# Repartitioning the routed experts of a transformer layer, and a separate path for the last batch

## The chip, the cores and the metric

One core of a Trainium2 chip runs the whole layer. The metric is the device time of one execution in microseconds (us), the median of several. PE is the tensor engine, PEld its weight loads, DVE the vector engine (VectorE), ACT the scalar engine (ScalarE), POOL GpSimd, SP the sync engine that issues most DMAs. Each engine runs its own list of instructions in order and waits on semaphores.

## The reference

`x` has 8 batches of 512 tokens of 128 values, in fp32. The layer is:

```python
x = x + attention(layernorm(x))
x = x + ffn(layernorm(x))

def attention(x):   # 16 heads
    y = einsum('bnd,hde->bhne', x, Wkqv) + bkqv       # k, q: 128 wide, v: 8 wide
    k, q, v = y[..., :128], y[..., 128:256], y[..., 256:]
    A = softmax(where(tril, q @ k.T / sqrt(128), -inf))
    return (A @ v, heads side by side) @ Wp + bp

def ffn(x):         # 8 experts of inner width 256, top 2 of a sigmoid router, and a shared expert
    shared = (silu(x @ shared_gate.T) * (x @ shared_up.T)) @ shared_down.T
    scores, idx = top_k(sigmoid(x @ router_w.T + routing_bias), 2); scores /= sum(scores)
    return shared + sum over the two experts e of score_e * (silu(x @ gate_w[e]) * (x @ up_w[e])) @ down_w[e]
```

## The kernel before

The program after a short preparation is one list of 215 slots `t` (`for t in range(SLOTS)` on each engine). Slots 0 to 127 project the 128 pairs of batch and head (`project`, three matmuls of 512 columns, since each operand is split into a high and a low fp16 half) and find row maxima (`score_for_max` on PE, `reduce_maxima` on DVE). Ten slots later (`LAG`) the pair's scores are made and exponentiated in three tiles (`score`, ACT line 1256), Pool masks the diagonals (lines 904 and 906), and every fourth slot (t = 15, 19, ...) `weigh_values` multiplies four heads with the values in fp32 (line 1032); ACT stores the products to `o_dram`. Attention so ends at slot 139. `FFN_AT` is 138.

For each batch a train of small steps follows, at slots that `STEPS` gives relative to 29 + 16 b: SP gathers sums and products from `o_dram` (`gather_products`, lines 796 and 797), DVE inverts the sums (`rinv`), SP stores the inverses and reads them back broadcast (`spread_inverses`, lines 801 and 806), Pool multiplies (`mult`, line 913), PE projects (`proj`), DVE adds and takes the variances by bn_stats and three Newton steps (`stats`, `aggr`, `newton0` to `newton2`), Pool normalizes (`norm`, line 920), ACT and DVE split the rows in two fp16 halves (`split`), SP stores them to `x_dram` and reads them back transposed (`turn_rows`, lines 810 and 819), and PE makes the logits of the router (`logits`, lines 1059 to 1061), of which ACT takes the exponential at once. Batch 7 has a table of its own, `LAST_STEPS`; its norm is on DVE.

Tokens are routed in three parts. `SPLITS` counts tiles of 128 tokens, four to a batch: (0, 8), (8, 20), (20, 32), that is 2, 3 and 3 batches. For each part DVE picks the two best experts of each token (`sort_at`, seven pieces, 13 operations, at two slots), PE counts and ranks them (`count`, `rank`), DVE turns ranks into rows (`place`), and Pool scatters the rows by indirect DMA into `xs_dram`, sorted by expert (`sends_at`, planned by `plan_sends`, line 929). SP reads them transposed, in quads of four tiles, into a ring of `X_RING` = 4 quads (line 865); for the first quad of a part it waits until all rows of the part are sent, and each quad waits for `gate_up` of the quad four before.

The feed-forward has 69 units, one in a slot from 138 to 206: 15, 19 and 19 of parts 0, 1 and 2 (each unit is 256 rows of one expert: 12 matmuls of 256 columns, lines 1099 to 1101) and 16 of the shared expert (each is half the inner width of a batch: 6 matmuls of 512 columns). The order was part 0, part 1, three shared batches, part 2, five shared batches (`ORDER`, `SHARED_ORDER`). ACT takes SiLU (line 1287) and the high half (1292), DVE the product (1546) and the low half (1549); `LATE` = 4 slots after its unit PE does the down-projection (lines 1135 to 1137). PE may be three units ahead (`DEEP`). ACT stores the experts' output to `ys_dram`. Pool gathers each token's two rows back by indirect DMA from slot `FETCH_AT` of the part on, three gathers in two slots (`plan_fetches`, lines 938 and 942), each pair waiting for `gate_up`. DVE adds the shared product of a batch (line 1541), and the weighted rows (`combine`, line 1517): tiles of all but the last part at planned slots, those of the last part after the slots. SP stores the output by batches in order (line 869).

One bank of PSUM (`bank_t`, bank 7) serves all small products in turn (`T_USES`, `turn`).

## Time and profile before

| | us |
|---|---|
| median of 3 runs | 767.33 (763.23 to 767.85) |
| the profiled execution | 765.89 |
| its span, first to last instruction | 764.1 |
| PE busy | 659.3 (86%) |
| VectorE busy | 538.8 (71%) |
| ScalarE busy | 459.9 (60%) |
| Pool busy | 304.5 (40%) |

The span is what the engines' rows cover; the profiled execution's own time is 1.8 us longer. Busy shares are means over stages that have different limits, so the rows below are read by stage.

### The profile page before, as it was taken

The numbers are of one execution on the slowest core, as the hardware profiler recorded it, in microseconds if no ns is written. First come the engines' busy times: TensorE is split into PE (matmuls) and PEld (weight loads), VectorE is DVE, ScalarE is ACT, GpSimd is POOL, SyncE is SP. The second block draws the span as 40 slices with busy tenths as digits, with TensorE's granted clock in tenths as the row PEclk, the third lists the DMA queues.
The fourth block names the chain that finished last, engine by engine and source line by source line (L and its number), as shares of the span: only waits on it lengthen the run. The fifth ranks groups of instructions, "written<-read, shape, count | busy, mean of one in ns | idle before, by whom it ended". The sixth has DMA issues, their size and how long they took to land. (4 is left out here: it accounts for less than half of the span.)

```text
span 764.1 us, 16403 instructions
## 1 busy us (share of the span) xinstructions
PE 659.3 (86%) x5426; PEld 398.2 (52%) x5426; DVE 538.8 (71%) x1900; ACT 459.9 (60%) x817; POOL 304.5 (40%) x508
## 2 busy tenths in 40 slices
PE   7478999999989998999999998996788789888920
PEld 6354455545545554454555554553377677577610
DVE  6799777787788788878778778762057755667914
ACT  3366667757757766667867766673475546556600
POOL 3493512314223223463322322367600067666671
PEclk9799999999999999999999999999899899999955
DMA  9102335411110311230210210134155543764322
GB/s 249 46 2 64 90 108 149 144 57 57 46 56 29 74 36 36 75 114 26 80 51 29 59 32 28 40 78 103 36 120 113 113 108 111 142 120 123 101 67 83
DMA packets 104849, 61.07 MB, mean 80 GB/s; under 512 B 45960, under 2 KB 96544, under 8 KB 104768
## 3 DMA queue, kind: packets, MB, share of 16 engines
q1 hardware_dynamic: 68336, 29.34, 15.9%
q10 hardware_dynamic: 32336, 22.29, 9.5%
q0 software_dynamic: 4096, 8.40, 4.3%
q8 instruction: 47, 0.77, 0.4%
q14 instruction: 34, 0.28, 0.1%
HBM read 19.88 MB, written 31.06 MB: 67 GB/s over the span
## 5 line engine op out<-in xcount | busy, mean ns | idle before, releaser
L1256 ACT ACTIVATE p_sb<-bank,inv_scale 128x512 f32<-128x512 f32 (+1 forms) x384 | 221.9, 614 | 34.3 <-PE bank L1018 27.1
L1370 DVE CUSTOM_DVE_ANT_0 junk<-bank,causal 128x512 bf16<-128x512 f32 (+3 forms) x512 | 221.2, 483 | 23.6 <-PE bank L995 23.3
L904 POOL TENSOR_SCALAR_AFFINE_SELECT p_sb<-p_sb 128x384 f32<-128x384 f32 x128 | 66.9, 522 | 303.5 <-ACT p_sb L1256 303.3
L1017 PE MATMUL bank<-ql,ah 128*128 128x512 f16 (+3 forms) x512 | 153.7, 300 | 0.0
L1018 PE MATMUL bank<-qh,al 128*128 128x512 f16 (+3 forms) x512 | 153.2, 300 | 0.0
L995 PE MATMUL bank<-ah,qh 128*128 128x512 f16 (+3 forms) x512 | 132.1, 302 | 23.6 <-DVE low L1370 22.2
L1016 PE MATMUL bank<-qh,ah 128*128 128x512 f16 (+3 forms) x512 | 147.5, 301 | 1.2 <-ACT p_sb L1256 1.2
L1342 DVE TENSOR_TENSOR ql<-bank,qh 128x512 f16<-128x512 f32 x128 | 88.5, 691 | 68.9 <-ACT qh L1221 65.2
L1221 ACT ACTIVATE qh<-bank 128x512 f16<-128x512 f32 x128 | 76.4, 597 | 63.3 <-PE bank L960 61.7
L1546 DVE SCALAR_TENSOR_TENSOR al<-bank,gu_scale,ah 128x512 f32<-128x512 f32 x69 | 51.6, 748 | 72.9 <-ACT ah L1287 56.6
L995 PEld LDWEIGHTS bank<-ah,qh 128*128 128x128 f16 x512 | 50.0, 98 | 82.2 <-DVE low L1370 49.7
L929 POOL DMA_INDIRECT xs_dram<-rows,place x64 | 65.8, 1028 | 60.4 <-DVE place L1507 41.0
L1287 ACT ACTIVATE ah<-bank,inv_gate 128x512 f32<-128x512 f32 x69 | 47.4, 687 | 62.8 <-PE bank L1101 44.6
L1032 PE MATMUL bank<-p_sb,v_sb 128*9 128x512 f32 (+3 forms) x1024 | 78.0, 446 | 7.3 <-POOL p_sb L906 7.3
L1016 PEld LDWEIGHTS bank<-qh,ah 128*128 128x128 f16 x512 | 50.2, 98 | 42.1 <-issue 9.5
L938 POOL DMA_INDIRECT p_sb<-ys_dram,place x57 | 59.4, 1042 | 30.6 <-issue 13.1
L1246 ACT ACTIVATE oT<-bank 128x512 f32<-128x512 f32 x32 | 19.1, 598 | 78.7 <-PE bank L1032 78.7
L1135 PE MATMUL bank<-wh,qh 128*128 (+1 forms) x276 | 52.7, 225 | 15.1 <-issue 7.3
L1099 PE MATMUL bank<-mh,wh 128*128 128x256 f16 x212 | 60.6, 286 | 3.7 <-issue 3.3
L1018 PEld LDWEIGHTS bank<-qh,al 128*128 128x128 f16 x512 | 50.2, 98 | 25.1 <-issue 0.4
L1100 PE MATMUL bank<-ml,wh 128*128 128x256 f16 x212 | 60.6, 286 | 2.7 <-issue 2.7
L1101 PE MATMUL bank<-mh,wl 128*128 128x256 f16 x212 | 60.5, 285 | 1.8 <-issue 1.7
(234 smaller groups left out, 1162.0 us busy)
## 6 DMA issues: line engine op xcount, KB each, us to landing
o_dram<-oT ACTq DMA_DIRECT2D x32, 256.0 KB, 2.3
ys_dram<-ql ACTq DMA_DIRECT2D x25, 256.0 KB
xs_dram<-causal ACTq DMA_DIRECT2D x6, 832.0 KB, 4.6
wst<-in_Wkqv SPq DMA_DIRECT2D x8, 264.0 KB, 5.3
x_sb<-in_x SPq DMA_DIRECT2D x8, 256.0 KB, 6.0
o_all<-o_dram SPq DMA_DIRECT2D x8, 256.0 KB
r_all<-r_dram SPq DMA_DIRECT2D x8, 256.0 KB
x_dram<-rows SPq DMA_DIRECT2D x8, 256.0 KB, 2.3
```

The costliest lines, as they stand in the source:

```text
L904: nc.gpsimd.affine_select(out=three, in_=three, compare_op=ALU.is_ge, fill=0.0, base=0, pattern=[[0, 3], [1, P]], channel_multiplier=-1).t ...
L929: nc.gpsimd.indirect_dma_start(out=m.xs_dram[g], out_offset=bass.IndirectOffsetOnAxis(ap=place[:, k, i:i + 1], axis=0), in_=rows[:, i // T ...
L995: last = nc.tensor.matmul(m.psum[M_BANK[n % 2]][:, at:at + w], qh[:, u % RING, i * P:(i + 1) * P], m.ah[:, seg(b, N, w)], start=True, stop ...
L1016: nc.tensor.matmul(bank, m.ah[:, keys], qh[:, s, c * P:N], start=True, stop=False)
L1017: nc.tensor.matmul(bank, m.ah[:, keys], ql[:, s, c * P:N], start=False, stop=False)
L1018: last = nc.tensor.matmul(bank, m.al[:, keys], qh[:, s, c * P:N], start=False, stop=True)
L1032: last = nc.tensor.matmul(m.psum[O_BANK][32 * j:32 * j + V1, c * P:N], m.v_sb[:, v // H * TB + c, v % H, :], p_sb[v % P_RING][:, P_AT[c]:P ...
L1099: nc.tensor.matmul(out, hi, x_h, start=True, stop=False)
L1221: nc.scalar.activation(qh[:, t % RING, :], m.psum[Q_BANK][:, :], ACT.Copy).then_inc(qh_ready, 1)
L1256: nc.scalar.activation(p_sb[v % P_RING][:, S_AT[k]:S_AT[k] + S_WIDTH[k]], m.psum[S_BANK[k]][:, 0:S_WIDTH[k]], ACT.Exp, scale=m.inv_scale[: ...
L1342: nc.vector.tensor_tensor(ql[:, t % RING, :], m.psum[Q_BANK][:, :], qh[:, t % RING, :], ALU.subtract).then_inc(ql_ready, 1)
L1370: last = nc.vector.tensor_tensor_reduce(out=junk[:, (3 * u + k) % 2, at:at + w], in0=m.psum[M_BANK[(3 * u + k) % 2]][:, at:at + w], in1=m. ...
```

## The change

- `SPLITS` becomes (0, 12), (12, 24), (24, 32): parts of 3, 3 and 2 batches, so 19, 19 and 15 units. All eight shared batches come behind the last part. Part 2 is at slots 176 to 190, the shared units at 191 to 206. The scatters of part 0 move from slots 76 to 83 to 88 to 99 (24 for 16), those of part 1 from 124 to 135 to 138 to 153, those of part 2 from 159 to 174 (24) to 157 to 167 (16). The 64 gathers move from slots 175 to 219 to 168 to 210. The last part's row additions after the slots are those of 8 tiles, not 12.
- Steps of batches 0 to 6: `rinv`, `mult` and `proj` two slots earlier, `aggr` and `newton0` in the slot of `stats`, `norm` three slots earlier, `split` and `logits` four slots earlier (batch 6's logits two, at 141). The exponential of batch 6's logits is taken with batch 7's, at slot 152; `lg` gets two buffers.
- The sorts of parts 0 and 1 are spread over five slots (`SORT_LATE`) instead of two.
- Batch 7: at slot 144 Pool itself issues the two gathers from `o_dram`, the store of the inverses and their broadcast, and waits for each in its own list. Its normalized rows are turned by four fp32 transposes on PE (slot 150, `late`), and ACT and DVE split them from PSUM straight into `xh` and `xl` (slot 151, `late_copy`); `x_dram` is not used for it. `split`, which makes the rows for the scatter, comes after the logits.
- SP: batch 6's rows are stored and turned at the fifth quad as before; the gathers, the broadcast and the turn of batch 7 are gone from its list.

```diff
...
 GU_BOUND = 32.0 / W_BOUND ** 2
-SPLITS = ((0, 8), (8, 20), (20, 32))
+SPLITS = ((0, 12), (12, 24), (24, 32))
 PARTS = len(SPLITS)
...
 PLACE_LATE = -(-(PV_AT - LOW_AT) // GROUP)
-STEPS = {"rinv": 2, "mult": 4, "proj": 6, "stats": 6, "aggr": 8, "newton0": 10, "newton1": 10, "newton2": 10, "norm": 11, "split": 14, "logits": 18}
-LAST_STEPS = {"rinv": 1, "mult": 4, "proj": 6, "stats": 6, "aggr": 6, "newton0": 7, "newton1": 7, "newton2": 7, "norm": 7, "split": 8, "logits": 13}
-PART_STEPS = {"sort": 22, "weigh": 26, "count": 27, "rank": 30, "place": 30, "expert": 34, "send": 31}
-LAST_PART_STEPS = {"sort": 14, "count": 16, "weigh": 16, "rank": 17, "place": 17, "expert": 18, "send": 18}
+STEPS = {"rinv": 0, "mult": 2, "proj": 4, "stats": 6, "aggr": 6, "newton0": 6, "newton1": 7, "newton2": 7, "norm": 8, "split": 10, "logits": 14}
+LATE_LOGITS = 16
+LAST_STEPS = {"rinv": 3, "mult": 3, "proj": 7, "stats": 7, "aggr": 7, "newton0": 8, "newton1": 8, "newton2": 8, "norm": 8, "late": 9, "late_copy": 10, "logits": 11, "split": 12}
+PART_STEPS = {"sort": 18, "weigh": 22, "count": 23, "rank": 26, "place": 26, "expert": 30, "send": 27}
+LAST_PART_STEPS = {"sort": 12, "weigh": 13, "count": 14, "rank": 15, "place": 15, "expert": 16, "send": 16}
+SORT_LATE = ((0, 0, 0, 1, 2, 3, 4), (0, 0, 0, 0, 1, 1, 1))
...
+    if (name, b) == ("logits", B - 2):
+        return step_at("rinv", b) - STEPS["rinv"] + LATE_LOGITS
     return PV_AT + H - GROUP + 2 + H * b + (STEPS if b < B - 1 else LAST_STEPS)[name]
...
-    return part_step_at("sort", g) + k // 4 * (GROUP if g < PARTS - 1 else 1)
+    return part_step_at("sort", g) + SORT_LATE[g == PARTS - 1][k]
...
     return next((b for b in range(B) if step_at(name, b) == t), None)
+
+
+def late_at(name, t):
+
+    return step_at(name, B - 1) == t
...
                 + [(SHARED_T_AT + k, "shared", k) for k in range(2)]
-                + [(step_at(name, b), name, b) for name in ("proj", "logits") for b in range(B)]
+                + [(step_at(name, b), name, b) for name in ("proj", "logits") for b in range(B)] + [(step_at("late", B - 1), "late", 0)]
                 + [(part_step_at(name, g), name, g) for name in ("count", "rank") for g in range(PARTS)])
...
 X_RING, GU_RING, LATE, DEEP = 4, 6, 4, 3
-ORDER = ("part", 0), ("part", 1), ("shared", 3), ("part", 2), ("shared", 5)
+ORDER = ("part", 0), ("part", 1), ("part", 2), ("shared", 8)
 SHARED_ORDER = (6, 5, 0, 7, 1, 2, 3, 4)
...
 quad_ends = [max(u + 1 for u, unit in enumerate(units) if unit.quad is quad) for quad in quads]
-LAST_TURN = next(q for q in range(X_RING, len(quads)) if FFN_AT + quad_ends[q - X_RING] >= step_at("split", B - 1))
 T_LAST = max(t for t, _, _ in T_USES)
...
-            def turn_rows(b):
+            def store_rows(b):
                 sp.wait_ge(xl_ready, b + 1)
                 sp.dma_start(m.x_dram[b * N:(b + 1) * N, :].rearrange("(t p) d -> p t d", p=P), rows[:, b % HN_RING, :, :]).then_inc(x_stored, 16)
+
+            def turn_rows(b):
                 sp.wait_ge(x_stored, 16 * (b + 1))
...
                         load_weights(e)
-                for b in range(B):
+                for b in range(B - 2):
                     if step_at("split", b) < LOW_AT + GROUP * g <= step_at("split", b) + GROUP:
+                        store_rows(b)
                         turn_rows(b)
...
                 if q == X_RING:
+                    store_rows(B - 2)
                     turn_rows(B - 2)
-                    gather_products(B - 1)
-                if q == X_RING + 1:
-                    spread_inverses(B - 1)
-                if q == LAST_TURN:
-                    turn_rows(B - 1)
                 if q >= X_RING:
...
+                if late_at("rinv", t):
+                    for k in range(2):
+                        pool.wait_ge(o_stored[k], 16 * H // GROUP // 2 * B)
+                    pool.wait_ge(rinv_ready, B - 1)
+                    pool.wait_ge(on_ready, B - 1)
+                    heads = m.o_dram[(B - 1) * H // GROUP * P:B * H // GROUP * P, :].rearrange("(h c) n -> h c n", h=H)
+                    pool.dma_start(sums[:, :], heads[:, DH, :]).then_inc(late_sums_placed, 16)
+                    pool.dma_start(o_all[:, :], heads[:, 0:DH, :]).then_inc(late_o_placed, 16)
+                    pool.wait_ge(rinv_ready, B)
+                    pool.dma_start(m.r_dram[(B - 1) * P:B * P, :], rinv[:, :]).then_inc(late_r_stored, 16)
+                    pool.wait_ge(late_r_stored, 16)
+                    inverses = m.r_dram[(B - 1) * P:B * P, :].rearrange("(h c) n -> h (c n)", h=H)
+                    pool.dma_start(r_all[:, :], inverses.unsqueeze(1).to_broadcast([H, DH, N])).then_inc(late_r_placed, 16)
+                if late_at("mult", t):
+                    pool.wait_ge(late_r_placed, 16)
+                    pool.wait_ge(late_o_placed, 16)
                 if (b := batch_at("mult", t)) is not None:
-                    pool.wait_ge(r_placed, 16 * (b + 1))
-                    pool.wait_ge(o_placed, 16 * (b + 1))
+                    pool.wait_ge(r_placed, 16 * min(b + 1, B - 1))
+                    pool.wait_ge(o_placed, 16 * min(b + 1, B - 1))
                     if b >= 1:
...
                     last.then_inc(t_filled, 1)
+                if late_at("late", t):
+                    turn("late", 0)
+                    pe.wait_ge(hn_ready, B)
+                    for i in range(TB):
+                        last = nc.tensor.transpose(bank_t[:, i * P:(i + 1) * P], hn[:, i, :], m.ident[:, :])
+                    last.then_inc(t_filled, 1)
                 if (b := batch_at("logits", t)) is not None:
...
                         pe.wait_ge(scale_chain, SCALE_LINKS)
-                    pe.wait_ge(x_turned, 16 * 2 * (b + 1))
+                    if b < B - 1:
+                        pe.wait_ge(x_turned, 16 * 2 * (b + 1))
                     for i in range(TB):
...
                 if unit.shared:
-                    if unit.half == 0:
+                    if unit.half == 0 and unit.batch < B - 1:
                         pe.wait_ge(x_turned, 16 * 2 * (unit.batch + 1))
+                    elif unit.half == 0:
+                        pe.wait_ge(t_taken, T_TURN["late", 0] + 1)
                     for kind, bank in ((0, GB), (1, UB)):
...
                     act.dma_start(m.ys_dram[quad.part][quad.rows, :].rearrange("(j p) d -> p j d", p=P), yst[:, q % X_RING, 0:quad.n * D].rearrange("p (j d) -> p j d", d=D)).then_inc(ys_stored[q % X_RING], 16)
+                if late_at("late_copy", t):
+                    act.wait_ge(t_filled, T_TURN["late", 0] + 1)
+                    act.wait_ge(wl_ready, KINDS * (E + 1))
+                    nc.scalar.activation(xh[:, seg(B - 1, N)], bank_t[:, :], ACT.Copy, scale=LIFT).then_inc(late_xh_ready, 1)
                 if t >= FFN_AT:
                     split_rows(t)
-                if (b := batch_at("logits", t)) is not None:
-                    act.wait_ge(t_taken, T_TURN["logits", b] + 1)
-                    nc.scalar.activation(ex[:, seg(b, TB), :], lg[:, :, :], ACT.Exp, scale=-1.0).then_inc(ex_ready, 1)
+                for b in range(B):
+                    if step_at("logits", max(b, B - 1) if b == B - 2 else b) == t:
+                        act.wait_ge(t_taken, T_TURN["logits", b] + 1)
+                        nc.scalar.activation(ex[:, seg(b, TB), :], lg[:, b % 2, :, :], ACT.Exp, scale=-1.0).then_inc(ex_ready, 1)
...
                     dve.wait_ge(t_filled, T_TURN["logits", b] + 1)
-                    if b >= 1:
-                        dve.wait_ge(ex_ready, b)
-                    nc.vector.scalar_tensor_tensor(out=lg[:, :, :], in0=bank_t[:, 0:TB * E].rearrange("p (t e) -> p t e", e=E), scalar=m.inv_logit[:, :],
+                    if b >= 2:
+                        dve.wait_ge(ex_ready, b - 1)
+                    nc.vector.scalar_tensor_tensor(out=lg[:, b % 2, :, :], in0=bank_t[:, 0:TB * E].rearrange("p (t e) -> p t e", e=E), scalar=m.inv_logit[:, :],
                                                    in1=m.rb_bc[:, :].unsqueeze(1).to_broadcast([P, TB, E]), op0=ALU.mult, op1=ALU.add).then_inc(t_taken, 1)
...
                     nc.vector.tensor_copy(ranks[:, 0:n], bank_t[:, 0:n]).then_inc(t_taken, 1)
+                if late_at("late_copy", t):
+                    dve.wait_ge(late_xh_ready, 1)
+                    dve.wait_ge(t_filled, T_TURN["late", 0] + 1)
+                    dve.wait_ge(wl_ready, KINDS * (E + 1))
+                    nc.vector.scalar_tensor_tensor(out=xl[:, seg(B - 1, N)], in0=bank_t[:, :], scalar=LIFT, in1=xh[:, seg(B - 1, N)], op0=ALU.mult, op1=ALU.subtract).then_inc(t_taken, 1)
                 if (b := batch_at("split", t)) is not None:
...
                 if (b := batch_at("rinv", t)) is not None:
-                    dve.wait_ge(sums_placed, 16 * (b + 1))
+                    if b < B - 1:
+                        dve.wait_ge(sums_placed, 16 * (b + 1))
+                    else:
+                        dve.wait_ge(late_sums_placed, 16)
                     if b >= 1:
...
                     nc.vector.reciprocal(rinv[:, :], sums[:, :]).then_inc(rinv_ready, 1)
...
```

## Rows read from the trace of the kernel before

**Rows 1.** stretches: busy us of each engine (instructions), granted clock, DMA share, GB/s

```profile
core 0: us, PE busy (x) PEld busy (x) DVE busy (x) ACT busy (x) POOL busy (x), PEclk, DMA share, GB/s
509.60:544.40 34.80, 26.46 (x209) 14.65 (x209) 6.65 (x35) 19.96 (x36) 26.61 (x40) 0.95 0.33 94
560.30:612.00 51.70, 41.45 (x423) 34.24 (x421) 33.87 (x89) 29.80 (x48) 1.27 (x1) 0.87 0.55 120
650.00:704.00 54.00, 46.56 (x499) 37.77 (x500) 35.18 (x64) 29.31 (x53) 34.48 (x34) 1.00 0.61 129
704.00:726.00 22.00, 21.39 (x210) 14.12 (x208) 20.50 (x42) 15.30 (x28) 14.28 (x14) 1.00 0.40 105
726.00:753.00 27.00, 6.06 (x35) 2.99 (x32) 3.46 (x9) 0.55 (x1) 17.37 (x19) 0.53 0.21 57
```

**Rows 2.** timeline, ScalarE's copies of slots 67 to 69, 87, 88 (start, duration)

```profile
271.78 0.60 ACT L1221 ACTIVATE qh<-bank 128x512 f16<-128x512 f32 x1
...
279.26 0.60 ACT L1221 ACTIVATE qh<-bank 128x512 f16<-128x512 f32 x1 [1.64 <-PE bank L960]
...
282.21 0.60 ACT L1221 ACTIVATE qh<-bank 128x512 f16<-128x512 f32 x1 [0.38 <-PE bank L960]
...
352.95 0.60 ACT L1221 ACTIVATE qh<-bank 128x512 f16<-128x512 f32 x1 [0.57 <-PE bank L960]
...
358.15 0.60 ACT L1221 ACTIVATE qh<-bank 128x512 f16<-128x512 f32 x1 [0.25 <-PE bank L960]
```

**Rows 3.** timeline, SiLUs of slots 143, 144, 159, 178, 180, 200, 201, 206

```profile
560.30 0.69 ACT L1287 ACTIVATE ah<-bank,inv_gate 128x512 f32<-128x512 f32 x1 [0.65 <-PE bank L1101]
...
568.03 0.69 ACT L1287 ACTIVATE ah<-bank,inv_gate 128x512 f32<-128x512 f32 x1
...
612.08 0.69 ACT L1287 ACTIVATE ah<-bank,inv_gate 128x512 f32<-128x512 f32 x1 [1.66 <-PE bank L1101]
...
660.59 0.69 ACT L1287 ACTIVATE ah<-bank,inv_gate 128x512 f32<-128x512 f32 x1 [4.35 <-remote]
...
667.20 0.69 ACT L1287 ACTIVATE ah<-bank,inv_gate 128x512 f32<-128x512 f32 x1 [4.30 <-PE bank L1101]
...
712.03 0.69 ACT L1287 ACTIVATE ah<-bank,inv_gate 128x512 f32<-128x512 f32 x1 [0.27 <-PE bank L1101]
...
713.99 0.69 ACT L1287 ACTIVATE ah<-bank,inv_gate 128x512 f32<-128x512 f32 x1 [0.48 <-issue]
...
724.41 0.69 ACT L1287 ACTIVATE ah<-bank,inv_gate 128x512 f32<-128x512 f32 x1 [0.28 <-PE bank L1101]
```

**Rows 4.** the chain of waits, its end (start, duration)

```profile
734.05 18.66 another core or an unknown queue
```

**Rows 5.** timeline, Pool's gathers of the last part: first and last of 24

```profile
718.66 0.94 POOL L938 DMA_INDIRECT p_sb<-ys_dram,place  x1 [3.75 <-PE bank L1101]
...
747.91 0.94 POOL L942 DMA_INDIRECT p_sb<-ys_dram,place  x1 [0.30 <-issue]
```

**Rows 6.** timeline, VectorE at the end

```profile
755.03 6.38 DVE L1517 SCALAR_TENSOR_TENSOR x_sb<-p_sb,weight,x_sb 128x128 f32<-128x128 f32 x24
```

**Rows 7.** timeline, PE's last group: first, 22nd and 23rd of 24

```profile
733.01 0.29 PE L1135 MATMUL bank<-wh,qh 128*128 128x128 f16 x1 [3.33 <-DVE qh L1549]
...
751.93 0.29 PE L1135 MATMUL bank<-wh,qh 128*128 128x128 f16 x1 [0.44 <-issue]
752.63 0.27 PE L1136 MATMUL bank<-wh,qh 128*128 128x128 f16 x1 [0.41 <-issue]
```

**Rows 8.** timeline, Pool between attention and feed-forward

```profile
544.12 3.13 POOL L920 TENSOR_SCALAR hn<-x_sb,stats,rstd 128x128 f32<-128x128 f32 x4
...
571.34 1.27 POOL L913 TENSOR_TENSOR onT<-o_all,r_all 128x512 f32<-128x512 f32 x1 [23.36 <-DMA r_all<-r_dram]
```

**Rows 9.** timeline, PE at the logits of batch 6

```profile
563.37 0.17 PE L1059 MATMUL bank<-rwh,xh 128*128 128x8 f16 x1 [2.44 <-DMA xl<-x_dram]
```

**Rows 10.** timeline, SP's broadcast of the inverses of batch 7

```profile
567.92 0.53 SPq L806 DMA_DIRECT2D r_all<-r_dram  x1
```

More of the change, by code:

```diff
@@ L715, in body @@
     tmp = sb("tmp2", [P, TB], F32)
-    lg = sb("lg", [P, TB, E], F32)
+    lg = sb("lg", [P, 2, TB, E], F32)
     ex = sb("ex", [P, TILES, E], F32)
@@ L753, in body @@
              "half_added", "out_ready", "out_stored",
-             "xn_ready", "xn_last_ready", "x_T", "ah_ready", "al_ready", "v_done", "v_ready", "mh_ready", "ml_ready", "scale_chain")
+             "xn_ready", "xn_last_ready", "x_T", "ah_ready", "al_ready", "late_xh_ready", "late_sums_placed", "late_o_placed", "late_r_stored", "late_r_placed", "v_done", "v_ready", "mh_ready", "ml_ready", "scale_chain")
     (q_done, qh_ready, ql_ready, max_scored, max_ready, low_stored, low_placed,
@@ L761, in body @@
      half_added, out_ready, out_stored,
-     xn_ready, xn_last_ready, x_T, ah_ready, al_ready, v_done, v_ready, mh_ready, ml_ready, scale_chain) = (sem(n) for n in names)
+     xn_ready, xn_last_ready, x_T, ah_ready, al_ready, late_xh_ready, late_sums_placed, late_o_placed, late_r_stored, late_r_placed, v_done, v_ready, mh_ready, ml_ready, scale_chain) = (sem(n) for n in names)
     o_stored = [sem(f"o_stored{k}") for k in range(2)]
```

## The prediction

> **What bounds the kernel now.** I read the views in this order: the stretches (busy time by stage), the end of the chain of waits, the SiLU rows of ScalarE as a clock of the feed-forward slots, and then the Pool and SP rows at the points where that clock stops. The span is 764.1 us, and the profiled execution took 765.89 us, 1.8 more. The reader is to see three regimes in [rows 1]. In attention PE sets the pace as long as there are projections: a plain slot takes 2.95 us and a slot with a value product 5.20 [rows 2]. In the last ten slots before the feed-forward (509.6 to 544.4) PE is busy 26.5 of 34.8 us and Pool 26.6: Pool's 18 scatters of part 1, two in a slot, hold the masks back. From slot 138 on PE issues the next unit as soon as it may. Undisturbed, a slot is 1.96 us (712.03 to 713.99 in [rows 3]), so 68 slots would take 133 us; they take 180 (544.4 to 724.41). After the last SiLU at 724.41 come 39.7 us in which almost nothing is computed: PE executes 35 matmuls in 27 us [rows 1], VectorE stands for 18.66 us in the chain [rows 4], Pool issues the last gathers at one in 1.25 us [rows 5], and 24 row additions of 6.38 us follow [rows 6].
>
> **The tail.** In the old plan part 2 (12 tiles, 24 gathers) is computed last but for five shared batches; its first gather runs at 718.66 and its last at 747.91 [rows 5]. In the new plan part 2 has 8 tiles and ends at slot 190, all eight shared batches stand behind it, and the 64 gathers are laid on slots 168 to 210 in place of 175 to 219. At most six gathers are left when the last but one gate/up product is done: 6 x 1.25 = 7.5 us from some 1.5 us before the last SiLU. VectorE has 16 additions left, 16/24 of 6.38 = 4.3 us. What stands between is PE. Its last down-projection is 24 matmuls, the first at 733.01 and the last but one at 752.63 [rows 7], against 1.31 us for such a group at full pace (an estimate: two undisturbed slots of 1.96 hold twelve matmuls of 512 columns and this group's 24 of 128, which are a third of the columns). Instructions start there 0.70 us apart (751.93, 752.63) or a multiple of it, for no wait that the profile shows. I have to say what makes this crawl. Rows for Pool as the cause: in 560.3 to 612, with Pool silent (one instruction), no such gap stands; they begin with the scatters at 613 and come in bursts through 650 to 704; and they are dense while gathers run back to back. Rows against: 704 to 726 has 14 Pool instructions and no gap at all (PE 21.4 of 22.0) [rows 1]. I take Pool as the cause. The crawl then ends with the last gather's landing. By 747.91 to 752.63 that is some 4 us after the last issue, so 7.5 - 1.5 + 4 = 10 us after the last SiLU; then a rest of the group, 1.5; the two additions of shared products, 1.5; row additions 4.3; output 2.9 (end of the additions 761.4 to 764.1). Tail: 20.2 us in place of 39.7, **-19.5**. If the crawl belongs to the last instructions of PE's program and not to Pool, it stays: then only 8 row additions (2.1) and a little are saved, -3.
>
> The Trainium skill ("Runtime: NRT & Kernel Launch", Instruction fetch mechanics) says that instruction fetch is mostly hidden and that PE holds some 2,048 instructions. By it the end of the program can't starve and the crawl is not the program's; the trace doesn't decide that. It goes with the choice above and changes no number.
>
> **Slots 128 to 137.** With part 1 ending at batch 5 as before, but its ranks known at slot 135 in place of 123, its 24 scatters move from slots 124 to 135 to 138 to 153. Pool is left with masks of about 0.8 us a slot, one product and one normalization (3.13 us [rows 8]) three slots earlier. The next limit is PE: 26.5 us of work in those slots, some of it waiting inside, or ScalarE with 20.0. I take 24 us for the ten slots (bounds 20 and 30): **-10.8**. **Start of the feed-forward.** At 544.12 the normalization of batch 6 stood ahead of the last masks; from 544.4 to 560.30 [rows 3] five slots took 15.9 us for 9.8. With it at slot 133 I leave 1 us: **-5**. **Logits of batch 6.** PE waited 2.44 us for the turned rows [rows 9] and ScalarE then loaded two tables; the slot took 7.73 us (560.30 to 568.03). Split at 135, logits at 141 with SP idle before it, and the exponential drawn to slot 152 remove all of it: **-5.7** (at least -4, as PE's order keeps its 12 small matmuls).
>
> **Attention.** Four slots (67, 71, 115, 119) carry 7 to 11 small VectorE operations at once: 279.26 - 271.78 = 7.48 against 5.20 [rows 2], 2.3 each; the rank and place slots add 1 to 1.5 each. In all about 14 us for two parts. The new sorts are spread over 79 to 83, and those of part 1 fall on 127 to 131, where VectorE has little else. Slot 83 gets stats, seed, sort and weights together (+2). I keep 5 of 14 for part 0: **-8** (bounds -2 and -11). The step table for each batch moves reciprocal and products two slots earlier and stacks stats, variance and the first Newton step; a wash: what slot 40 loses, slots 33, 35 and 36 gain. The gathers of products are issued at the same point of SP's list, and land about 2 us ahead of the new reciprocal, so no new wait.
>
> **Batch 7.** Removed are SP's two gathers, the store and the broadcast, x_dram's store and two turns. Added are four Pool DMAs, four fp32 transposes on PE and two copies. Pool reaches slot 144 at about gate_up 5, one scatter behind; it waits for the reciprocal, for the store and for the broadcast before it goes on, and everything behind it, 15 scatters of part 1, waits too. No row shows a plain Pool DMA. Its issue I put at the indirect one's 1.25 us [rows 5]; the flight of the broadcast at SP's, issue 567.92 to product 571.34, 3.4 us [rows 8, 10]. Lower bound: as on SP (0.5 us of issue); upper: 2 us of issue and 5 of flight each. Sum from Pool at slot 144: 1.25 + 2.5 (sums), 0.5 reciprocal (VectorE is there at the same time, +2), 1.25 + 2, 1.25 + 3.4, 1.27 product: 15 us, against 5 slots or so of PE (144 to 148, 11 us with its own stalls). PE's projection waits **+3** (0 to +12). Transposes, copies and their bubbles cost **+1.5**; the round trip through x_dram that they replace lay under slots 149 to 153 and gives nothing back by itself, but the last place is ready two slots earlier. The stalls of the chain from projection to place (560.30 to 612.08, 16 slots, 51.8 us for 31.4, of which logits of batch 6 are counted above) stay: the Newton steps, the table loads, the sorts. The 15 scatters that Pool still owes after the product need 15 x 1.28 = 19 us and are done as PE comes to slot 157, which the chain itself makes late: 24 scatters in the feed-forward bring bursts, of which I take **+3** outside other stalls.
>
> The Trainium skill ("DMA: Bandwidth & Descriptors", Latency and other measured facts) speaks against this move: first byte about 0.6 us on SP's path and 1 us on Pool's. By that alone four transfers would lose 1.6 us on the chain; no row here shows it, and the 3 above doesn't contain it.
>
> **Part 2 and the gathers.** 16 scatters for 24, at 0.4 us each (612.08 to 667.20: 55.1 us for 21 slots, 14 over, with 24 scatters and ten gathers in them): **-3**. The SiLUs of slots 178 and 180 began after 4.35 and 4.30 us of idle on ScalarE (660.59, 667.20), because part 2's rows were sent until 650; in the new plan they are sent by slot 168 for slot 176: **-5**. From 667.20 to 724.41 26 slots took 57.2 us, 6.2 over, with 1.5 gathers in each; 12 more slots carry them now: **+4**.
>
> **Sum.** -19.5 -10.8 -5 -5.7 -8 +3 +1.5 +3 -3 -5 +4 = -45.5 us from 765.9: 720.4. The profiled execution lies 1.4 us below the median of 767.33, so the forecast for the median is **722 us**.
>
> **Rivals.** (1) The crawl stays. For it: the gaps keep a beat of 0.70 us whatever Pool's beat is, PE's program ends there, and 704 to 726 shows Pool without crawl. The tail gives -3 in place of -19.5: **738 us**. (2) The chain of batch 7 is late on Pool. The waits at slot 144 reach the upper bound, the scatters of part 1 are pushed behind slot 157, and PE stands for them: +9 and +6: **737 us**. (3) The change does not do what it says in attention: the slots 128 to 137 are bound by the ping-pong of scores and exponentials near 3 us a slot, and stats, variance and Newton in slots 35 and 36 take back what the sorts gave: +6 and +8, **736 us**. (4) Slower: Pool becomes the bound of the whole feed-forward. It has 40 scatters and 64 gathers after slot 138 in place of 88 DMAs and the four waits; they need 104 x 1.28 = 133 us of 180. It decides only if the blocked time at slot 144 passes 15 us and each Pool DMA then costs PE 0.7 us more than now: 104 x 0.7 = 73, 722 + 73 - 20 = **775 us**.
>
> **Chances.** Forecast 0.58, with its own range 708 to 733; rivals (1) 0.17, (2) 0.08, (3) 0.09, (4) 0.03; 0.05 is left for a mixture near no change. The range 705 to 744 leaves out 2 in 10: the lower end adds 4 in attention, 4 in slots 128 to 137, and a last group of PE that doesn't crawl at all (8); the upper takes in rivals 1 to 3 with some room. What a measurement of this kernel tells from no change is about 1%, 8 us. Faster by more: 0.92; within: 0.04; slower: 0.04.
>
> **What would show it.** The first SiLU near 525 us, and that of slot 143 some 11 us later; no table load for an exponential before slot 152; Pool's product for batch 7 within 3 us of PE's need; unit 206's SiLU near 700; the last gather issued 6 us after it and the end 20 us after it. Wrong would be: gaps of 0.70 us after the last gather has landed, PE waiting at slot 157 for transposed rows, or the ten slots before the feed-forward still above 3 us each.

## The result, and the profile after

The changed kernel takes 742.18 us (740.01 to 742.48, 4 runs) against 767.38 us: a ratio of 0.967, 95% interval 0.9632 to 0.9708. It is faster, inside the forecast range of 705 to 744, and 20 us above the 722 that I forecast. The profiled execution took 742.48 us, its span is 740.7. Of all executions in this document one is left out: one of the four with denser scatters (below) took 958.41 us at a mean granted clock of 0.652, against 0.963 to 0.967 in the other three.

Three stretches, cut at the first and the last SiLU, against the terms of my sum (from 764.1 of span to 740.7):

| stretch | before | after | difference | my terms |
|---|---|---|---|---|
| start to first SiLU (slot 138) | 544.4 | 533.3 | -11.1 | -18.8 |
| first to last SiLU (slot 206) | 180.0 | 186.8 | **+6.8** | -7.2 |
| last SiLU to the end | 39.7 | 20.6 | -19.1 | -19.5 |

The tail came out as long as I had worked out; the feed-forward, where I expected a gain, got longer. One profile fixes these stretches to some us only: a second one of the same kernel (744.52 us, the first run on the first kind below) has 531.5, 193.5 and 17.7. The feed-forward is longer than before in both, by 6.8 and 13.5 us. By stretches of the kernel after (busy us of each engine and its instructions; PEclk is the granted clock), to be held against [rows 1]:

```profile
core 0: us, PE busy (x) PEld busy (x) DVE busy (x) ACT busy (x) POOL busy (x), PEclk, DMA share, GB/s
502.20:533.30 31.10, 29.50 (x265) 16.38 (x261) 17.22 (x72) 22.68 (x39) 13.47 (x30) 1.00 0.34 86
533.30:561.80 28.50, 24.39 (x273) 19.54 (x266) 16.75 (x33) 14.65 (x27) 14.31 (x16) 1.00 0.51 120
564.00:576.00 12.00, 5.05 (x32) 3.00 (x33) 2.87 (x14) 1.06 (x2) 7.46 (x9) 0.66 0.19 59
606.90:686.70 79.80, 69.71 (x733) 59.17 (x734) 45.83 (x81) 44.34 (x79) 49.26 (x48) 0.94 0.62 132
720.10:740.70 20.60, 6.11 (x65) 4.72 (x62) 12.18 (x33) 1.95 (x4) 6.66 (x7) 0.61 0.42 115
```

The first line runs from slot 127 to the first SiLU, one slot more than the first line of [rows 1]; the same cut takes 40.0 us in the kernel before, with Pool busy for 29.4. Pool's work has become 13.5 us and PE is busy in 29.5 of 31.1, so the scatters no longer hold the masks back and PE is the limit. The third line is a new loss: 32 matmuls in 12 us. Pool's rows and, with them, the two SiLUs of slots 149 and 150 (start, duration; in brackets the idle time before and what ended it):

```profile
546.66 0.61 POOL L921 DMA_DIRECT2D sums<-o_dram  x1
547.28 0.56 POOL L922 DMA_DIRECT2D o_all<-o_dram  x1
551.54 0.58 POOL L924 DMA_DIRECT2D r_dram<-rinv  x1 [3.70 <-DVE rinv L1471]
554.47 0.53 POOL L927 DMA_DIRECT2D r_all<-r_dram  x1 [2.35 <-DMA r_dram<-rinv]
557.87 1.27 POOL L936 TENSOR_TENSOR onT<-o_all,r_all 128x512 f32<-128x512 f32 x1 [2.87 <-DMA r_all<-r_dram]
559.30 1.39 POOL L952 DMA_INDIRECT xs_dram<-rows,place  x1 [0.16 <-issue]
561.00 0.99 POOL L952 DMA_INDIRECT xs_dram<-rows,place  x1 [0.30 <-issue]
...
572.41 0.96 POOL L952 DMA_INDIRECT xs_dram<-rows,place  x1 [0.30 <-issue]
```

```profile
559.29 1.13 PE L1072 MATMUL bank<-wp,onT 128*128 128x128 f32 x8 [0.72 <-POOL onT L936]
```

```profile
561.76 0.69 ACT L1319 ACTIVATE ah<-bank,inv_gate 128x512 f32<-128x512 f32 x1 [2.86 <-PE bank L1131]
575.54 0.69 ACT L1319 ACTIVATE ah<-bank,inv_gate 128x512 f32<-128x512 f32 x1 [10.87 <-remote]
```

The chain of batch 7 on Pool, which I feared, costs PE 0.72 us of waiting. Then Pool works off its scatters, eleven back to back, most of them 1.27 us apart. PE waits once for VectorE in that time (1.21 us), and then does this, for no wait that the profile shows ("issue"):

```profile
568.98 0.42 PE L1129 MATMUL bank<-mh,wh 128*128 128x256 f16 x1
569.81 0.37 PE L1130 MATMUL bank<-ml,wh 128*128 128x256 f16 x1 [0.41 <-issue]
570.53 0.37 PE L1131 MATMUL bank<-mh,wl 128*128 128x256 f16 x1 [0.36 <-issue]
571.95 0.38 PE L1129 MATMUL bank<-mh,wh 128*128 128x256 f16 x1 [1.05 <-issue]
```

After the first row starts are 0.83, 0.72 and 1.42 us apart, then 2.11 and 1.43, mostly close to multiples of 0.70: the crawl of [rows 7], now in the middle of the kernel, and 13.8 us from one SiLU to the next. The tail, which answers to [rows 4 to 7]:

```profile
720.12 0.69 ACT L1319 ACTIVATE ah<-bank,inv_gate 128x512 f32<-128x512 f32 x1
```

```profile
727.64 0.95 POOL L961 DMA_INDIRECT p_sb<-ys_dram,place  x1 [0.30 <-issue]
```

```profile
728.84 0.75 DVE L1586 SCALAR_TENSOR_TENSOR x_sb<-bank,inv_down,x_sb 128x512 f32<-128x512 f32 x1 [4.31 <-remote]
...
733.02 0.75 DVE L1586 SCALAR_TENSOR_TENSOR x_sb<-bank,inv_down,x_sb 128x512 f32<-128x512 f32 x1 [1.39 <-PE bank L1169]
733.69 4.29 DVE L1562 SCALAR_TENSOR_TENSOR x_sb<-p_sb,weight,x_sb 128x128 f32<-128x128 f32 x16
```

```profile
730.25 0.29 PE L1167 MATMUL bank<-wh,qh 128*128 128x128 f16 x1 [3.72 <-DVE qh L1594]
```

The last gather is issued 7.5 us after the last SiLU (forecast 6), the 16 additions take 4.29 us (forecast 4.3), the end comes 20.6 us after that SiLU (forecast 20). The way there is not quite the one forecast: PE's last group starts 10.1 us after that SiLU (forecast 10) because it waits for VectorE, which itself sits idle for 4.31 us until a release that the profile doesn't name ("remote"), and it then runs without a gap.

### The profile page after: what moved, and what is told of

The parts are those of the page before. It is cut to its first block, busy times and chain, and to the rows that moved or that the text cites. A ratio compares the mean times of both kernels' runs of the same rounds, so it can differ in the third digit from the quotient of the medians.

```text
span 740.7 us, 16412 instructions
## 1 busy us (share of the span) xinstructions
PE 656.3 (89%) x5430; PEld 399.1 (54%) x5430; DVE 539.9 (73%) x1901; ACT 457.5 (62%) x816; POOL 307.4 (42%) x512
## 3 DMA queue, kind: packets, MB, share of 16 engines
q1 hardware_dynamic: 66144, 28.22, 15.9%
q10 hardware_dynamic: 32336, 22.29, 10.1%
## 4 chain that ended last, share of the span: by engine, by line
PE 56%; DVE 19%; ACT 7%; issue 6%; another core or an unknown queue 6%; POOL 1%; ACTq 1%; DMA 0%; DVEq 0%; POOLq 0%
PE bank L1018 8%; PE bank L1039 7%; PE bank L1055 6%; PE bank L1041 6%; PE bank L1040 6%; DVE junk L1412 5%; PE bank L981 3%; PE bank L983 3%; PE bank L982 3%; DVE ql L1384 3%; PE bank L1131 2%; PE bank L1129 2%; ACT qh L1253 2%; PE bank L1130 2%
## 5 line engine op out<-in xcount | busy, mean ns | idle before, releaser
L1288 ACT ACTIVATE p_sb<-bank,inv_scale 128x512 f32<-128x512 f32 (+1 forms) x384 | 221.9, 614 | 39.7 <-PE bank L1041 32.0
L1384 DVE TENSOR_TENSOR ql<-bank,qh 128x512 f16<-128x512 f32 x128 | 88.5, 692 | 63.8 <-ACT qh L1253 60.3
L961 POOL DMA_INDIRECT p_sb<-ys_dram,place x64 | 66.9, 1045 | 35.6 <-issue 13.7
L1055 PE MATMUL bank<-p_sb,v_sb 128*9 128x512 f32 (+3 forms) x1024 | 74.9, 433 | 0.3 <-POOL p_sb L913 0.3
L1167 PE MATMUL bank<-wh,qh 128*128 (+1 forms) x276 | 54.3, 229 | 10.9 <-DVE qh L1594 4.9
L1040 PEld LDWEIGHTS bank<-ql,ah 128*128 128x128 f16 x512 | 50.1, 98 | 21.5
```

What stands on the lines that cost most here:

```text
L1040: nc.tensor.matmul(bank, m.ah[:, keys], ql[:, s, c * P:N], start=False, stop=False)
L1055: last = nc.tensor.matmul(m.psum[O_BANK][32 * j:32 * j + V1, c * P:N], m.v_sb[:, v // H * TB + c, v % H, :], p_sb[v % P_RING][:, P_AT[c]:P ...
L1288: nc.scalar.activation(p_sb[v % P_RING][:, S_AT[k]:S_AT[k] + S_WIDTH[k]], m.psum[S_BANK[k]][:, 0:S_WIDTH[k]], ACT.Exp, scale=m.inv_scale[: ...
L1384: nc.vector.tensor_tensor(ql[:, t % RING, :], m.psum[Q_BANK][:, :], qh[:, t % RING, :], ALU.subtract).then_inc(ql_ready, 1)
```

## Experiments

The chips turned out to be of two kinds. On the **first kind** (three sessions, the result's among them) the kernel before takes 766 to 768 us; on the **second kind** (two chips) 744. No chip was met in two sessions, so chip and session aren't told apart; "kind of chip" is short for both. Each experiment is read against kernels of its own kind. Slots are told by the start of their SiLU.

**Second kind** (kernel before: 744.54 us, 742.77 to 746.07, 7 runs).

*Batch 7's transfers on SP again*: the Pool block at slot 144 out, and in SP's list

```diff
                 if q == X_RING:
                     store_rows(B - 2)
                     turn_rows(B - 2)
+                    gather_products(B - 1)
+                if q == X_RING + 1:
+                    spread_inverses(B - 1)
-LAST_STEPS = {"rinv": 3, "mult": 3, ...
+LAST_STEPS = {"rinv": 1, "mult": 4, ...
```

> The kernel after, with the four transfers of batch 7 back on SP (reciprocal at slot 142, product at slot 145); all else stays. Theory 1 (Pool, blocked for 12 us by its own waits, owes 12 scatters and issues them in one unbroken run from 559.3 to 573.4, and PE crawls as long as that run lasts): no run of more than a few scatters is left, the gap of 13.8 us ahead of the SiLU of slot 150 shrinks to 4 to 5, and the kernel is 8 to 11 us faster than after, 731 to 734 us. Rival (the 13.8 us are those of the chain itself, the Newton steps and the fp32 transposes on PE): the gap stays over 10 us and the time stays within 3 us of 742.

Measured: 703.46 us, ratio 0.9445 (0.9419 to 0.947). That is far below every figure of mine, and its trace has no run of gaps of 0.70 us: from the first to the last SiLU PE has one idle stretch of 0.3 us or more for no wait, of 1.22 us. I had nothing to compare it with before the changed kernel itself ran on this kind.

*Without the 16 scatters of batches 4 and 5* (their rows are left out of the output):

```diff
+                    if i // TB in (4, 5):
+                        continue
                     nc.gpsimd.indirect_dma_start(out=m.xs_dram[g], ...
```

> The kernel after without the 16 scatters of batches 4 and 5 (their rows are left out of the experts' input, and nobody waits for them). Theory 1: with no run of scatters behind the product, PE has no gaps of 0.70 us between slots 149 and 157, slot 149 to 150 takes 4 to 5 us and the run is 9 to 12 us shorter than after. Rival (the chain itself): slot 149 to 150 stays above 10 us.

Measured: 707.33 us, one run. Slot 149 still takes 8.9 us: PE waits 3.36 us for Pool's product, so on this kind the chain on Pool is late by that much, with or without scatters behind it. The crawl that this edit was to test isn't there to be taken away on this kind.

*Ten transfers more on Pool in the kernel before*, at slot 151, where its Pool is silent; once indirect, once plain (64 KB each):

```diff
+                if t == 151:
+                    pool.wait_ge(gate_up, 13)
+                    for j in range(10):
+                        nc.gpsimd.indirect_dma_start(out=m.scratch, ..., in_=rows[:, 2, 0, :], in_offset=None)   # or pool.dma_start(m.scratch[...], rows[:, 2, 0, :])
```

> The kernel before with ten more indirect scatters, of rows that nobody reads again, into a scratch tensor, back to back at slot 151, where Pool is silent and PE has no gap of this kind. Theory 1 (dense indirect transfers of Pool make PE crawl): gaps of 0.70 us on PE between about 589 and 604 us, and 5 to 12 us more for the whole kernel. Rival (PE crawls by its own program at that place, and Pool's run only coincides): no new gap, time within 2 us of before.

> As the run with ten more indirect scatters, but ten plain Pool transfers of the same 64 KB each. If the cost lies in Pool's queue as such, the same gaps come; if it lies in the indirect form or in its duration of issue, none or few, and the time is within 2 us of before. I expect fewer gaps, since the batch 7 transfers of the kernel after show none beside them.

Measured: 743.05 and 742.73 us, one run each, as the kernel before there, and no new gap. On the second kind ten dense transfers of Pool cost PE nothing that shows. These two traces also stand for the kernel before on this kind.

**First kind** (kernel before: 765.78 us, 763.71 to 767.02, 7 runs). *The changed kernel again*:

> The changed kernel itself, on whatever chip this call gets. Theory (the PE's gaps of 0.70 us beside Pool's scatters belong to the first chip, not to the kernel): on the chip of the experiments so far, 705 to 710 us, that is 35 to 40 us under the kernel before there (744.5), the slots 149 to 150 take 4 to 9 us instead of 13.8, the tail behind the last SiLU 20 us as on the first chip. Rival (the gaps come with the changed kernel's own order of Pool's transfers and its program on PE): the gaps are there again and the time is 720 to 742 us.

Measured: 742.0 us (740.59 to 744.52), ratio 0.9687 (0.9662 to 0.9713), the gaps and 13.6 us for slot 150 as in the result. The pattern belongs to kernel and kind of chip, not to one execution. From the first to the last SiLU PE's idle stretches of 0.3 us and more for no wait are 21 before (10.0 us) and 30 and 34 in the two profiles of the changed kernel (21.8 and 24.7 us); on the second kind they are one before (1.0) and one after (1.7).

*Steps as far apart as before* for batches 0 to 6 and parts 0 and 1, but for one: `LATE_LOGITS` stays, so batch 6's logits stay at slot 141 while its rows are split at slot 139, four slots later than in the changed kernel. The kernel before had the logits at 143:

```diff
-STEPS = {"rinv": 0, "mult": 2, "proj": 4, "stats": 6, ... "split": 10, "logits": 14}
+STEPS = {"rinv": 2, "mult": 4, "proj": 6, "stats": 6, ... "split": 14, "logits": 18}
-PART_STEPS = {"sort": 18, ... "send": 27}
+PART_STEPS = {"sort": 22, ... "send": 31}
```

> The changed kernel with the steps of batches 0 to 6 and of parts 0 and 1 as far apart as in the kernel before (rinv 2 ... logits 18, sort 22 ... send 31). Theory (drawing them together gave little, the attention's gain was 2.2 us to slot 127): within 3 us of the changed kernel. Rival (my forecast's term, 8 us of the attention from this): 7 to 10 us slower than the changed kernel, all of it lost before slot 128.

Measured: 751.81 us, 9.8 slower than the changed kernel on the same chip, and neither theory has the place right. The first SiLU is at 531.66 against 531.52, and slot 3 had begun 2.3 us later (42.32 against 39.99), so the steps are worth nothing in attention; from slot 3 on the old ones are 2.2 us shorter. The loss comes at slot 142, where PE waits for batch 6's rows on their way through DRAM (the slot takes 11.5 us for 3.3):

```profile
546.68 0.17 PE L1089 MATMUL bank<-rwh,xh 128*128 128x8 f16 x1 [6.80 <-DMA xl<-x_dram]
```

The logits start 6.6 us after the issue of the rows' store here (540.08 to 546.68) and 6.3 in the kernel before (557.09 to 563.37), and this run leaves them two slots for it where the kernel before left four. So it shows that logits at slot 141 need the split at 135; it doesn't give the worth of the steps against the kernel before, whose wait there was 2.44 us [rows 9]. That is the term I had booked as "logits of batch 6", not the one called "attention".

*The old order of the feed-forward*:

```diff
-ORDER = ("part", 0), ("part", 1), ("part", 2), ("shared", 8)
+ORDER = ("part", 0), ("part", 1), ("shared", 3), ("part", 2), ("shared", 5)
```

> The changed kernel with the order of the FFN before (part 0, part 1, three shared batches, part 2, five shared batches). Theory (the tail is a train of Pool's gathers that starts when part 2's rows are stored): part 2 is done 6 slots later, so its 16 gathers of 1.30 us start 2 to 4 us before the last SiLU in place of lying wholly ahead, the last is issued 16 to 18 us after that SiLU in place of 9, and the kernel is 6 to 9 us slower than the changed one. Rival (Pool's train is dense from part 2's scatters on, so that it sets the end in either order): within 2 us of the changed kernel.

Measured: 750.18 us, 8.2 slower. The last SiLU is where it is in the changed kernel (724.42 and 725.05), the last gather is issued at 736.7, 12.2 us after it, for 2.6 in the changed kernel there, and the end comes 25.0 us after it for 17.7. The mechanism of the tail holds, though the last gathers of both kernels came 4 to 6 us earlier after that SiLU than I had said: the order alone is worth 7 of the 22 us by which the tail there is shorter than before.

*Scatters in the feed-forward two to a slot*, with SP's transfers for batch 7: `at += 3` for `at += 3 if at < 6 * FFN_AT else 4`.

> The version with batch 7's four transfers on SP, with part 1's and part 2's scatters two to a slot in place of three to two slots. Theory (the end is the place tables of part 2, plus 80 transfers of Pool at 1.30 us, plus 10 us): the place tables are no earlier, the time stays at 701 to 706 us. Rival (part 1's rows all sent four slots sooner takes waits off the PE at slots 150 to 157): 695 to 700 us. Against both: batch 7's product on Pool waits behind two more scatters, 2.6 us, which would give 706 to 708 us.

Measured: 747.14 us (745.55 to 748.39, 3 runs), 5 slower than the changed kernel. The expectation was written in figures of the second kind and the chip was of the first, so they can't be held against it. Two things differ from the changed kernel, the scatters and SP's transfers, and what each costs there is not shown; the two together don't help.

**Second kind again** (kernel before: 743.96 us, 740.58 to 745.21, 7 runs). *The changed kernel, and the version with SP's transfers, in pair*:

> The changed kernel once more, in pair with the next run. On a chip of the first kind (kernel before at 766): 742 us. On one of the second kind (kernel before at 744.5): theory (no gaps of 0.70 us there, the rest as on the first): 704 to 709 us, slots 149 to 150 with the 4 to 9 us of a late product. Rival (the whole gain is the same 25 us on either chip): 718 to 722 us.

> The version with batch 7's four transfers on SP, the same file as the first experiment, in pair with the changed kernel. Theory (Pool's transfers for batch 7 cost little either way): within 4 us of the changed kernel on either chip. Rival (with SP's transfers Pool has its scatters done sooner and the product comes in time): 6 to 12 us faster than the changed kernel. Rival on a chip of the first kind: the gaps of 0.70 us take it all back and it is 2 to 6 us slower.

Measured: 706.81 us, ratio 0.9494 (0.9476 to 0.9511), and 704.21 us, 0.9455 (0.9431 to 0.948). So the gain is 37 us here and 24 to 25 on the first kind. Four stretches of the changed kernel here:

```profile
501.20:532.10 30.90, 29.31 (x265) 16.40 (x261) 16.85 (x72) 22.48 (x39) 13.37 (x29) 1.00 0.34 86
532.10:561.50 29.40, 25.72 (x271) 21.13 (x264) 17.58 (x41) 15.02 (x27) 16.19 (x18) 0.90 0.50 121
592.40:654.20 61.80, 61.61 (x749) 57.23 (x747) 47.07 (x82) 45.32 (x80) 47.47 (x48) 1.00 0.81 172
684.90:705.80 20.90, 4.18 (x72) 3.84 (x69) 10.98 (x31) 1.84 (x3) 9.29 (x9) 0.75 0.43 119
```

The third line (slots 159 to 190) is the same work as the fourth line of the first fence, with the same 48 transfers of Pool: 61.8 us for 79.8, PE without a gap, at a higher rate of transfer (172 GB/s for 132). At batch 7's chain PE now arrives earlier and does wait for Pool:

```profile
555.43 1.26 POOL L936 TENSOR_TENSOR onT<-o_all,r_all 128x512 f32<-128x512 f32 x1 [4.33 <-DMA r_all<-r_dram]
```

```profile
556.84 2.04 PE L1072 MATMUL bank<-wp,onT 128*128 128x128 f32 x8 [3.68 <-POOL onT L936]
```

With SP's transfers the product of that version ran at 548.80 in its first profile, 6.6 us sooner, and PE waits instead 3.06 us for the normalized rows (1.68 in the changed kernel):

```profile
561.69 0.63 PE L1065 MATMUL bank<-ident,hn 128*128 128x128 f32 x4 [3.06 <-DVE hn L1476]
```

The last SiLU is 3.9 us earlier and the end 2.6, which is 0.4%: one wait for another. The rival "6 to 12 us" falls. Whether moving the transfers to Pool pays on the first kind was not measured by itself.

*Without the 48 gathers of batches 0 to 5* (these batches' output lacks the experts' rows), on the second kind and on the first (kernel before: 767.96, one run):

```diff
+                    if i // TB < 6:
+                        continue
                     nc.gpsimd.indirect_dma_start(out=yg(i)[:, k, :], ... in_=m.ys_dram[g], ...
-                    dve.wait_ge(fetched[b], 16 * 2 * TB)
+                    if b >= 6:
+                        dve.wait_ge(fetched[b], 16 * 2 * TB)
```

> The changed kernel without the 48 gathers of batches 0 to 5 (their rows of the output get what lies in the buffer in place of the experts' rows; the additions stay). The scatters before slot 167 and the last 16 gathers stay. On a chip of the first kind: theory (Pool's dense indirect transfers bring on the gaps of 0.70 us): slots 168 to 192 take 1.98 us each, 50 us in place of some 60, the time is 728 to 734 us. Rival (the gaps belong to PE's program, each some two microseconds behind an instruction page): slots 168 to 192 take 60 us as before, 740 to 743 us. On a chip of the second kind all slots take 1.98 us in any case, and the time is that of the changed kernel within 3 us, as the last gather stays where it is.

> The kernel of the run before again (the changed one without the gathers of batches 0 to 5), in the hope of a chip of the first kind. In the kernel before on the first chip the slots run as on the second kind of chip until Pool's first transfer of the FFN (613.57 us) and are broken up by gaps of 0.70 us from there on. Theory (on such a chip Pool's dense indirect transfers bring the gaps on): slots 168 to 192 at 1.98 us each, 48 us in place of 61 to 63, the rest as in the changed kernel, 728 to 732 us in all. Rival (the gaps come with something else that begins there, the quads of the parts on PE): slots 168 to 192 take 58 to 63 us, 740 to 743 us. On a chip of the second kind: 701 to 704 us, and nothing is told apart.

Measured: 702.8 us on the second kind, 4 under the changed kernel where I allowed 3; **723.28 us** on the first, 19 under it (one run each). In the latter, slots 159 to 168 (scatters still there) and slots 169 to 190 (Pool silent), and below them the last SiLU of the second stretch:

```profile
605.40:628.10 22.70, 19.10 (x202) 16.17 (x203) 11.21 (x17) 12.75 (x24) 13.18 (x13) 0.92 0.59 122
629.60:671.40 41.80, 41.61 (x505) 38.58 (x503) 33.28 (x62) 30.56 (x55) 0.00 (x0) 1.00 0.63 133
```

```profile
671.35 0.69 ACT L1321 ACTIVATE ah<-bank,inv_gate 128x512 f32<-128x512 f32 x1 [0.29 <-PE bank L1133]
```

Slots 169 to 190 take 41.7 us (629.62 to 671.35) for 52.9 in the changed kernel (633.84 to 686.74) and 41.9 on the second kind (612.21 to 654.16). From slot 171 to slot 200 no slot is off the undisturbed pace. The gathers of batches 6 and 7 start at 689.8, and the next SiLUs stand 3.85 and 3.64 us apart for 2.64 and 1.30. The rival, that the gaps belong to PE's program, is out. Nor is it that PE has less traffic beside it: the stretch without gathers moves 133 GB/s, slots 159 to 190 of the changed kernel 132. The 728 to 732 that I expected was too high by 5 to 9 us. The tail is 15.5 us here, 5 less than in the result's profile and 2 less than in the second one, whose first SiLU stands where this one's does (531.52 and 531.51); the rest lies in the feed-forward, 174.4 us for 186.8 and 193.5.

## Why the forecast was right, and where its sum was not

Sign and range were right, and the range in part by luck. 742.2 lies outside my own range of 708 to 733, in room that was there for rivals 1 to 3 (736 to 738), and no rival is what happened: what went wrong is a term that I had in the sum at a few us. Of the signs that I had named, the last SiLU came at 720.1 for "near 700" and the first at 533.3 for "near 525". The sum held -45.5 us; the result is -25 on the first kind (-24 when run again) and -37 on the second. The stretches of the second kind (kernel before from the run with ten plain transfers, whose time is the same; the other such run has 543.0, 163.0 and 35.3) separate the plan from the crawl:

| | first kind: before, after | second kind: before, after |
|---|---|---|
| start to first SiLU | 544.4, 533.3 (-11.1) | 540.3, 532.1 (-8.2) |
| first to last SiLU | 180.0, 186.8 (+6.8) | 165.3, 152.8 (-12.5) |
| last SiLU to the end | 39.7, 20.6 (-19.1) | 35.3, 20.9 (-14.4) |

- **The mis-sized term is "bursts, of which I take +3".** By the excess of the first kind over the second, the crawl costs 180.0 - 165.3 = 14.7 us in the feed-forward before and 186.8 - 152.8 = 34.0 after (40.7 by the second profile), so 19.3 more (26.0) where I charged all moves of part 1's, part 2's and the gathers' transfers with 3 - 3 + 4 = 4. The 34.0 is net of 3 us that PE waits less for Pool at batch 7 on the first kind. Half of it could be read from the kernel before: its Pool has no scatter in the feed-forward until 613.57 us, and up to slot 158 its SiLUs advance as on the second kind (64.1 and 63.8 us from slot 138). The new plan puts 24 scatters of part 1 into exactly that clean stretch, and batch 7's wait on Pool bunches eleven of them into an unbroken train. There the excess grows by 9.7 us: 4.0 to slot 148 (24.4 us for 20.2 on the second kind) and 5.7 from there to slot 158 (43.9 for 38.2, the train among them). I had said that the chain's own stalls would cover them. The other 9.6 us lie behind slot 158, where the excess is 24.0 us with 73 transfers of Pool up to the last SiLU, and was 14.4 with 69; why nearly as many cost more there is not shown.
- **The cause that I chose for the crawl was right**, and the choice kept rival 1 (738) from being the forecast. It is shown for the first kind by taking the gathers away; by what way they slow PE is open. **The tail** (-19.1 for -19.5) owes more to the gathers' plan than to the crawl: the last gather is issued 7.5 us after the last SiLU for 23.5 before, and on the second kind, where PE's crawl is absent, the tail still shrinks by 14.4 us, with that gather at 10.8 for 25.4. From the last gather to the end pass 9.9 us before and 10.1 after on the second kind, 16.2 and 13.1 (15.0 by the second profile) on the first. That the term came within 0.4 us is luck: the second profile gives -22.0. On the second kind the gathers end the tail, as the last eight additions show:

```profile
698.24 2.19 DVE L1562 SCALAR_TENSOR_TENSOR x_sb<-p_sb,weight,x_sb 128x128 f32<-128x128 f32 x8 [4.39 <-DMA p_sb<-ys_dram,place]
```

- **Attention, -8, was wrong.** To slot 127 the changed kernel gained 2.2 us (2.8 from slot 3 on, 3.4 by the second profile), and the run with the old steps shows that drawing the steps together gives nothing there. The sorts' slots gain as I said (5.4 us over slots 68 to 81, 5.6 over 116 to 121), but slots 82 to 102 lose 7.5 again: 3.8 up to slot 88, ahead of the first scatter of part 0 at 361.75, and the rest beside its 24 scatters. Rival 3 had a loss of this size (+8) that takes back what the sorts gave, but laid it on slots 35 and 36; slots 34 to 38 lose 1.4. Its other half, slots 128 to 137 bound near 3 us each, did not come.
- **Slots 128 to 137, -10.8, came to -8.9** (31.1 us for 40.0 from slot 127 to the first SiLU, so 25.9 for the ten slots that I put at 24): PE, not Pool, is the limit. **Start of the feed-forward**: -2 for -5 (13.8 us for 15.9 to slot 143), since slot 139 still takes 6.5 us on the first kind (3.4 on the second). **Logits of batch 6**: no wait is left, as said; slot 144 takes 1.6 us.
- **Batch 7 on Pool**: 0.72 us of wait on the first kind (1.27 in the second profile), 3.7 on the second, for +3. **Quads of part 2**: the stops at slots 178 and 180 are gone on both kinds, as said.

The balance on the first kind: -45.5, attention +5.8, slots 128 to 137 +1.9, start of the feed-forward +3, tail +0.4, batch 7's wait -2.3, and the crawl 19.3 - 4 = +15.3 make -21.4; the spans give -23.4. So 2 us are not assigned to a term, or 5 if the crawl is taken gross of the 3 us above.

The Trainium skill ("Runtime: NRT & Kernel Launch", Instruction fetch mechanics) had fetch mostly hidden. By it the crawl was not to come from PE's program, and the stretch without gathers agrees, with PE busy for 41.6 of 41.8 us; whether it is PE's fetch that Pool's transfers hold up on the first kind, no run shows. The other rule that I drew on from the Trainium skill ("DMA: Bandwidth & Descriptors", Latency and other measured facts), a first byte later on Pool's path than on SP's, is not to be seen on the first kind: the broadcast takes 3.4 us from issue to product on Pool (554.47 to 557.87) as on SP [rows 8, 10]. On the second kind it takes 4.85 us on Pool (550.58 to 555.43; 4.4 in the run without 16 scatters) and 3.4 and 4.0 in two profiles of the version on SP, a difference in the direction of the rule.

## What to carry to other kernels

When a transfer train is moved, look at what the stretch that it enters looks like without any, and charge it by the worst stretch beside such a train, not by the mean of a mixed one. Even that falls short here: with nearly as many transfers behind slot 158 the excess grew from 14.4 to 24.0 us. When an engine issues on a fixed beat for no wait that the profile shows, compare stretches in which each other queue is silent: here that view of the kernel before points at the cause, and taking the transfers away shows it. A queue that waits in its own list saves up its work and then releases it in one train.

## What the runs showed of the hardware

- Chips, or sessions, differ. The kernel before takes 766 to 768 us on one kind and 744 on the other, the changed one 742 and 707. Slots 138 to 150 of the kernel before, with Pool all but silent, take the same on both to 0.3 us in 39 (38.8 and 38.6).
- On the first kind PE, beside Pool's back-to-back indirect transfers (one in 1.25 to 1.27 us), starts instructions mostly some 0.70, 1.40 or 2.10 us apart, in bursts: 5.05 us of matmuls in 12, with the granted clock at 0.66 there. It stops when these transfers are left out (41.6 of 41.8 us busy). In attention 24 such transfers bring on no idle stretch of PE of 0.3 us or more for no wait, and the first SiLU is at 533.3 and 531.5 on the first kind and 532.1 on the second. What in the chip does it stays open, the issue or the descriptors or the data of these transfers; plain transfers of Pool were tried only on the second kind, where nothing crawls.
- Issue of a plain transfer on Pool takes 0.53 to 0.61 us, an indirect one 0.95 in most cases (1.2 to 1.5 in 19 of the changed kernel's 128 on the first kind) and a pause of 0.30.
